# Latent queries of the first attention: three fp32 matmuls become nine fp16 ones, and the projections run one head earlier

## What is computed

```python
B, S = 8, 256; DIM_Q, H, K, D_C, D_CQ, R = (256, 16, 128, 64, 192, 64)
q_big = einsum('bshk,hkq->bshq', (hidden_q @ Wq.T).reshape(B, S, H, K), w_kc_q)
q_big = apply_rope(q_big, sin_q, cos_q)
kv_r  = apply_rope(kv_c, sin_k, cos_k)
q_r, k_r = einsum('bshq,hqr->bhsr', q_big, W_qr), einsum('bld,hdr->bhlr', kv_r, W_kr)
attn  = softmax(einsum('bhsr,bhlr->bhsl', q_r, k_r))
ctx_c = einsum('bhsl,bld->bhsd', attn, kv_r)
ctx   = einsum('bhsd,hkd->bhsk', ctx_c, w_kc_kv)   # then @ Wo.T
```

## Time and profile before

| what | value |
|---|---|
| median of 3 runs | 1660.24 us (1660.09 to 1660.62) |
| the profiled execution's own time | 1660.06 us |
| its span, first to last instruction | 1658.1 us |
| mean granted clock of TensorE | 0.983 of full speed |
| PE busy | 1589.3 us (96% of the span) |
| DVE busy | 1305.9 us (79%) |
| POOL busy | 1021.2 us (62%) |
| ACT busy | 1013.7 us (61%) |

### The profile page before, as it was taken

How to read it: one execution, slowest core, us unless ns; L and a number is a source line. 1 busy time by engine, 2 the same in 40 slices (tenths; PEclk the granted TensorE clock), 3 DMA queues, 4 the chain that set the end, 5 groups by cost and what they waited for, 6 DMA issues and landing times. The chain is left out here.

```text
span 1658.1 us, 48690 instructions
## 1 busy us (share of the span) xinstructions
PE 1589.3 (96%) x16127; PEld 1299.1 (78%) x16127; DVE 1305.9 (79%) x3044; ACT 1013.7 (61%) x2024; POOL 1021.2 (62%) x970
## 2 busy tenths in 40 slices
PE   5889999999999999999999999999899899999998
PEld 4668888888888888888888888888786445556787
DVE  6988888888888888888888888888783578885223
ACT  5876767676777676767676777676222466664121
POOL 5348888888888888888888888788100224431321
PEclk8699999999999999999999999999999999999999
DMA  9721121121122122112112114412940011101244
GB/s 257 252 78 44 51 78 44 46 83 46 45 72 59 40 65 63 47 51 79 40 54 79 43 51 112 86 44 81 219 85 0 7 42 65 65 8 53 100 148 160
DMA packets 184808, 125.97 MB, mean 76 GB/s; under 512 B 107562, under 2 KB 171992, under 8 KB 184368
## 3 DMA queue, kind: packets, MB, share of 16 engines
q1 hardware_dynamic: 183216, 121.27, 26.5%
q0 software_dynamic: 1536, 3.99, 0.7%
HBM read 81.98 MB, written 24.48 MB: 64 GB/s over the span
## 5 line engine op out<-in xcount | busy, mean ns | idle before, releaser
L1178 POOL TENSOR_TENSOR c_rest<-c_prob 128x1024 f16<-128x1024 f32 (+1 forms) x513 | 801.4, 1572 | 209.1 <-ACT c_prob L966 186.5
L1071 DVE TENSOR_REDUCE c_mxp<-c_psM 128x1 f32<-128x400 f32 (+1 forms) x1040 | 581.8, 572 | 98.1 <-PE c_psM L785 86.5
L966 ACT ACTIVATE c_prob<-c_psS,ln,c_exp_scale 128x1024 f32<-128x1024 f32 (+1 forms) x514 | 536.4, 1044 | 193.7 <-PE c_psS L801 188.7
L801 PE MATMUL c_psS<-c_q,c_kk 128*128 128x256 f16 (+1 forms) x3350 | 512.8, 272 | 0.1
L819 PE MATMUL c_psV<-c_vb,c_prob 128*128 128x129 f16 (+1 forms) x3328 | 428.8, 221 | 1.2 <-ACT c_acc L1020 1.2
L822 PE MATMUL c_psV<-c_vb,c_rest 128*128 128x65 f16 (+1 forms) x3328 | 401.0, 193 | 0.0
L801 PEld LDWEIGHTS c_psS<-c_q,c_kk 128*128 128x128 f16 (+1 forms) x3350 | 312.6, 99 | 69.1 <-issue 0.3
L785 PE MATMUL c_psM<-c_kkm,c_q 128*128 128x400 f16 (+1 forms) x1040 | 346.1, 333 | 4.4 <-DVE c_mxp L1071 3.0
L822 PEld LDWEIGHTS c_psV<-c_vb,c_rest 128*128 128x128 f16 (+1 forms) x3328 | 303.4, 98 | 33.4
L819 PEld LDWEIGHTS c_psV<-c_vb,c_prob 128*128 128x128 bf16 (+1 forms) x3328 | 313.6, 97 | 9.4 <-ACT c_acc L1020 1.4
L747 PE MATMUL c_psQ<-c_xb,c_w2s 128*128 128x256 f16 x1188 | 162.7, 274 | 6.9 <-PEq L163 4.8
(11 more groups left out here) (323 smaller groups left out, 2188.5 us busy)
## 6 DMA issues: line engine op xcount, KB each, us to landing
c_w2s<-w_scr SPq DMA_DIRECT2D x66, 256.0 KB, 2.6
c_ms<-m_scr SPq DMA_DIRECT2D x67, 192.0 KB, 2.3
c_w2s<-w_scr SPq DMA_DIRECT2D x66, 128.0 KB, 2.0
acc_scr<-c_acc SPq DMA_DIRECT2D x129, 64.0 KB
kv<-acc_scr SPq DMA_DIRECT2D x16, 512.0 KB, 6.6
m_w<-in_L_ffn_W SPq DMA_DIRECT2D x16, 352.0 KB, 3.5
c_vb<-V SPq DMA_DIRECT2D x27, 129.0 KB, 2.0
c_kk<-KK SPq DMA_DIRECT2D x27, 128.0 KB, 2.0
```

What stands on the lines that cost most here:

```text
L801: mm = pe.matmul(psS[g % 2][0:r, i * S:(i + 1) * S], src[:, (lo + i) * P:(lo + i) * P + r], mov[slot][:, :], start=(one == 0 and i % 2 == ...
L966: nc.scalar.activation(prob[g][0:r, 0:w], psS[g % 2][0:r, 0:w], ACT.Exp, bias=keep["ln1024"][0:r, :], scale=exp_scale[slot][0:r, :]).then_ ...
L1071: nc.vector.tensor_reduce(mxp[:, st, c:c + 1], psM[:, st, 0:CHUNKS[c][1]], AX.X, ALU.max).then_inc(mx_done, 1)
L1178: nc.gpsimd.tensor_tensor(rest[g][0:r, 0:w], prob[g][0:r, 0:w], high[0:r, 0:w], ALU.subtract).then_inc(rest_done, 1)
```

## The change

What it does, part by part:

- `m`'s pair matrix is kept as high and low fp16 halves (scaled by 256, `M_UP`), in the same 192 KB. In the preparation ScalarE makes the high halves, GpSimd the low ones, in two parts each, and twelve stores take the place of six.
- The turned projection `roped` is split into fp16 `ropedH` (ScalarE, `rope_high`) and `ropedL` (GpSimd, `rope_low`).
- `q_lat` becomes `q_lat_high` (six matmuls: both halves of `m` with `ropedH`) and `q_lat_low` (three, with `ropedL`). All are fp16 of 256 columns, at the end of the even step.
- `q_first` runs one head earlier, in the odd step, into the unused half of `psS[1]`; `q_second` goes to the even step. `cos_first` writes a new SBUF tile `ropeA`, so `add_first` reads `ropeA` and `ropeB`, both in SBUF, where it had read `psQ` and `ropeB`.
- VectorE does `turn_first` and `cos_first` in the odd step, and `turn_second`, `cos_second`, `add_first`, `add_second` in the even one.
- `q_high` moves ahead of the shift's copy in the odd step, `q_other` into the same step. SyncE's waits move with all of it.

```diff
@@ phase_prepare: SyncE, GpSimd, ScalarE, VectorE
-            sp.wait_ge(m_scaled, 1)
+            mp = m2.rearrange("p t (g u) e d -> p t g u e d", u=2)
+            scr = t["m_scr"].bitcast(F16)
             for e in range(2):
+                for part, ready in ((0, m_high), (1, m_low)):
+                    sp.wait_ge(ready, e + 1)
+                    c0, c2 = (2 * e + part) * P, (4 + part) * P
+                    sp.dma_start(scr[:, 0:HALF, c0:c0 + DC].rearrange("g p d -> p g d"),
+                                 mp[:, part, :, 0, e, :]).then_inc(m_stored, 16)
...
+            sp.wait_ge(m_stored, 16 * 12)
+            for e in range(2):
+                pool.wait_ge(m_high, e + 1)
+                nc.gpsimd.tensor_tensor(m2[:, 1, :, e, :], m[:, :, e, :], m2[:, 0, :, e, :],
+                                        ALU.subtract).then_inc(m_low, 1)
...
             nc.scalar.activation(warm[:], eps[:], ACT.Exp)
+            for e in range(2):
+                act.wait_ge(m_scaled, e + 1)
+                nc.scalar.activation(m2[:, 0, :, e, :], m[:, :, e, :], ACT.Copy).then_inc(m_high, 1)
@@ TensorE
             def q_second(p, maxima_of=None):
                 pe.wait_ge(in_wR, 16 * (p + 1))
-                pe.wait_ge(ropedA, p + 1)
+                pe.wait_ge(turnA, 3 * p + 3)
+                if not isinstance(p, int) or p > 0:
+                    pe.wait_ge(ropedR, p)
+                    pe.wait_ge(ql_done, 2 * p)
...
-                for e in range(3):
-                    mm = pe.matmul(psQ[:, S:2 * S], ms[:, e, :], roped[:, e, :], start=(e == 0), stop=(e == 2))
+            def q_lat_high(p):
+                pe.wait_ge(rh_done, 2 * p + 2)
+                pe.wait_ge(in_m, 16 * (p + 1))
+                for e in range(3):
+                    for part in range(2):
+                        pe.matmul(psQ[:, S:2 * S], msp[:, e, part, :], ropedH[:, e, :],
+                                  start=(e == 0 and part == 0), stop=False, skip_group_check=True)
+
+            def q_lat_low(p):
+                pe.wait_ge(rl_done, 2 * p + 2)
+                for e in range(3):
+                    mm = pe.matmul(psQ[:, S:2 * S], msp[:, e, 0, :], ropedL[:, e, :],
+                                   start=False, stop=(e == 2), skip_group_check=True)
...
+            q_first(2, 0, psV)
+            q_first(2, 1, psV)
...
+                    if u % 2 == 1:
+                        q_first(p + 1, 0, ahead_q)
                     values(n, 0, (0, 1))
-                    if u % 2 == 0:
-                        q_first(p, 0)
                     maxima(n + 2, p2, 0, s2)
                     values(n, 0, (1, 2))
-                    if u % 2 == 0:
-                        q_first(p, 1, maxima_of=n + 1)
+                    if u % 2 == 1:
+                        q_first(p + 1, 1, ahead_q, maxima_of=n + 1)
                     else:
                         q_second(p, maxima_of=n + 1)
...
                     values(n, 3)
+                    if u % 2 == 0:
+                        q_lat_high(p)
                     scores(n + 1, 2, s1, (0, 6))
+                    if u % 2 == 0:
+                        q_lat_low(p)
@@ ScalarE
+                        rope_high(p, slice(0, 2), ropedA)
+                        rope_high(p, slice(2, 3), ropedR)
@@ VectorE
-                nc.vector.tensor_tensor(psQ[:], psQ[:], tabA[:, 0:2 * S], ALU.mult).then_inc(turnA, 1)
+                nc.vector.tensor_tensor(ropeA[:], src[:, 0:2 * S], tabA[:, 0:2 * S], ALU.mult).then_inc(turnA, 1)
...
-                nc.vector.tensor_tensor(roped[:, 0:2, :].rearrange("p e s -> p (e s)"), psQ[:],
+                nc.vector.tensor_tensor(roped[:, 0:2, :].rearrange("p e s -> p (e s)"), ropeA[:],
                                         ropeB[:, 0:2, :].rearrange("p e s -> p (e s)"), ALU.add).then_inc(ropedA, 1)
...
-                    if u % 2 == 1:
-                        add_second(p)
-                    for k in range(2, 6):
-                        reduce_max(n + 2, k)
                     if u % 2 == 0:
                         add_first(p)
+                    reduce_max(n + 2, 2)
+                    if u % 2 == 0:
+                        add_second(p)
+                    for k in range(3, 6):
+                        reduce_max(n + 2, k)
@@ GpSimd
+                    if u % 2 == 0:
+                        p = (AHEAD // 2) * j + (AHEAD + u) // 2
+                        rope_low(p, slice(0, 2), 1)
+                        rope_low(p, slice(2, 3), 2)
```

155 lines of the change are left out of this document (96 added, 59 removed).

## The result

The changed kernel takes 1720.49 us (median of 4 runs, 1719.90 to 1720.93), the kernel before 1660.43 us beside it (4 runs, 1660.09 to 1661.56): 1.036 times as long, 95% interval 1.0342 to 1.0378. The forecast was 1718 us, slower. The profiled execution took 1720.93 us with a span of 1719.1 us, 61.0 us more than the span before.

A forecast was written before the change was run, and what follows sets the result against it. TensorE, busy throughout the loop, was taken as the bound, with VectorE's late places deciding the change. 1660.1 + 46.7 (loop) + 9.8 (preparation) + 1.3 (extra `q_first`) = 1718 us, range 1694 to 1740.

The forecast's parts named there:

- TensorE's gain: Loop: nine fp16 matmuls (0.98 us) replace six fp32 passes (1.37 us), saving 0.39 us a pair.
- The three waits: Even step: TensorE waits for VectorE 0.23 us at the shift, 0.52 at the fifth, 0.21 at the sixth maxima matmul.
- The addition against GpSimd: Even step: `add_first`, now with two SBUF operands, waits for GpSimd's small instruction, adding 0.16 us a pair.
- The loop: All 64 pairs: waits and the addition's delay, less TensorE's gain, +0.73 us a pair, 46.7 us in all.
- The preparation: Ahead of the loop: high halves, low halves, twelve stores and a load start the next block 9.8 us later.
- The entry to the loop: Ahead of the loop: a third `q_first` adds twelve matmuls, 1.3 us.
- 2 (the addition meets no one): Loop: the addition misses GpSimd's instructions, so +0.57 us a pair and 1708 us; chance 20%.
- 3 (GpSimd as bound): Loop: GpSimd's added work costs more or the addition meets long instructions; 0.5 us more a pair, 1750 us; chance 10%.
- 4 (stores cost little): Preparation: stores are issued as soon as halves are ready and the barrier is late anyway; 1709 us; chance 8%.
- 5 (stalls half as large): Loop: VectorE catches up in the odd step, so +0.3 us a pair and 1690 us; chance 6%.
- 6 (nine matmuls not cheaper): Loop: the nine matmuls take 0.152 us each, costing the old 1.37 us; 1743 us; chance 2%.
- Rival 1 (VectorE keeps up): Loop: TensorE stays the bound and the kernel gets faster, 1646 us; chance 4%.

The follow-up runs named there:

- run 4: Kernel before with only the three fp32 latent matmuls exchanged for nine fp16 ones in place, halves left out: 1634.63 us, ratio 0.9869.
- Run 1: Changed kernel with VectorE's first addition behind the third reduction instead of the second, second addition behind the fourth: 1692.21 us, ratio 1.0218.
- run 3: Changed kernel with the loop's first addition reading its left operand from PSUM instead of SBUF, roped first parts left out: 1705.18 us, ratio 1.0286.
- run 8: Changed kernel with TensorE's order refitted, `q_low` behind the fifth reduction, high halves early and weights' low halves on VectorE in the preparation: 1664.52 us, ratio 1.0017.
- run 6: Changed kernel without GpSimd's low halves of the roped queries; the low matmuls read the high halves instead: 1720.14 us, ratio 1.0359.
- run 12: Kernel of run 11 with TensorE's fourth maxima matmul of the even step two groups later: 1645.52 us, ratio 0.9921 of the kernel before.
- run 11: Kernel of run 9 plus an early dummy GpSimd tensor_tensor in the preparation, and eight value matmuls moved ahead of the even step's shift: 1654.56 us, ratio 0.9994.
- run 9: Kernel of run 8 with `q_low` split behind the odd step's fifth and sixth reductions instead of whole behind the fifth: 1662.90 us, ratio 1.0027.

## Why the prediction was right

It was right in time, sign and mechanism. Of 57.8 us forecast and 61.0 measured, the two smallest terms, the entry to the loop and the part behind it, were missed most (by 1.7 and 2.9), and the preparation's error of 1.1 the other way hides a part of that. The terms, one by one:

- **TensorE's gain**, 0.39 a pair: 0.38, by run 4 alone.
- **The three waits**, 0.23 at the shift, 0.52 + 0.16 at the fifth and 0.21 at the sixth maxima matmul, +0.73 with the gain: 0.25, 0.69 and 0.20 in the median; four heads give +0.765. Run 1 shows that the place of the addition makes the largest of them. The due times of TensorE and VectorE's starts, carried over from the steps before, held to 0.07 us in the pair shown.
- **The addition against GpSimd**, 0.16: run 3 gives 0.20. Its partners were named only in part. It waits for the small `rest` instruction, as said (in 41 of the 47 pairs from 200 to 1000 us, in the others for a long one near its end), and gives its delay on to GpSimd's sum behind it, which the prediction did not count; that one has no one waiting.
- **The loop**, 46.7: 46.4. This agreement is partly luck: 0.765 x 63.5 is 48.6, and the loop before had one turn of four heads that took 34.50 instead of 32.88, which the changed kernel does not have.
- **The preparation**, 9.8: 8.7. The first three stores were sent behind the first high half, the next three behind the first low half and the rest without a pause; the load began at 83.62 instead of 84.7. One premise failed: GpSimd did not wait for VectorE's last addition, it began 0.7 earlier (74.49 instead of 75.2), behind the first high half. The two held each other up, and GpSimd's halves took 4.98 instead of 3.8 and ended at 79.47 instead of 79.0. The last three stores went out at 80.11 behind the three ahead of them, so this end did not set the time. Other executions of the same preparation end up to 1.7 us later, so the forecast lies inside what the traces show.
- **The entry to the loop**, 1.3: 3.0. The step that failed in size: it counted only the twelve matmuls, not that the halves of the first two pairs add their own waits and the first steps their stalls (0.44 us at 116.70, until VectorE has read the projection in `psS[1]`, and 0.48 at 122.75, for a reduction).
- **Behind the loop**, 0: 2.9. The code there is the same. TensorE waits 1.81 us for VectorE until 1234.89, where it waited 0.46. The sixteen matmuls behind that wait take 3.01 us instead of 2.23, and the sixteen behind those 4.56 instead of 3.67, with the granted clock at 0.50 (1.2 GHz) from 1236.2 to 1239.5; in the same place before it was 1.00. These three are the whole 2.9. The clock fell 1.3 us behind the end of the wait; that the longer wait brought it down is not shown, and why that wait differs was not tried. The other kernels lie between 4.4 less (run 4) and 5.4 more (run 8) than the kernel before in the part behind the loop, so this part belongs to no change.

Of the rivals, 2 (the addition meets no one) falls by run 3, 3 (GpSimd as bound) by run 6, 4 (stores cost little) by the block's start at 84.65, 5 (stalls half as large) by the distances above, 6 (nine matmuls not cheaper) by run 4. Rival 1 (VectorE keeps up) is false for the kernel as changed. What the prediction did not consider is that the waits need not be there: run 12 does the same arithmetic with other orders, and a shorter preparation, and ends 13 us under the kernel before.

## What to carry to other kernels

When one engine is full, ask of each instruction that it waits for whether its producer is asked at a place where it has had time: VectorE was busy 87% before and 84% after, and still cost 1.1 us a pair. A wait that is filled comes back at the next place if the producer has no pause in between, as in run 11, and stays away if it has one, as in run 12. Removing one wait can also bring out another that it covered, as in run 9. And shift an addition's operand from PSUM to SBUF only after looking what GpSimd does beside it.
